# Each turn of the probabilities paired with a ternary product, and its scaling moved ahead of the sums, in an attention and ternary feed-forward kernel

## What is computed

```python
q = x + braak_embed[stage][..., None]            # one bias for each row
attn = softmax(einsum('bsd,btd->bst', q, f))     # scores against f, softmax over t
y = einsum('bst,btd->bsd', attn, f)              # the same f as values
xh = y @ H                                       # Hadamard matrix, 256 x 256
scale = clip(max|xh| over the row, 1e-5) / 7
xq = clip(round(xh / scale), -8, 7) * scale      # 4-bit codes
wq = ternary(weight) * mean|weight| of its row   # -1, 0, 1
out = x + einsum('bsi,oi->bso', xq, wq)
```

## Time and profile before

| | |
|---|---|
| median of three runs | 104.96 us |
| span of the profiled execution, first to last instruction | 102.9 us |
| rest of the time, before and after the span | 2.1 us |
| PE busy (matmul) | 96.4 us, 94% |
| PE's weight loads | 91.0 us, 88% |
| DVE busy | 87.0 us, 85% |
| ACT busy | 76.2 us, 74% |
| POOL busy | 48.5 us, 47% |
| DMA transposes of the codes | 13, 2.4 to 3.8 us from issue to landing |

### The profile page before, as it was taken

How to read it: one execution, slowest core, us unless ns; L and a number is a source line. 1 busy time by engine, 2 the same in 40 slices (tenths; PEclk the granted TensorE clock), 3 DMA queues, 4 the chain that set the end, 5 groups by cost and what they waited for, 6 DMA issues and landing times.

```text
span 102.9 us, 2603 instructions
## 1 busy us (share of the span) xinstructions
PE 96.4 (94%) x801; PEld 91.0 (88%) x801; DVE 87.0 (85%) x221; ACT 76.2 (74%) x196; POOL 48.5 (47%) x72
## 2 busy tenths in 40 slices
PE   5999999999999999999999999999999999999640
PEld 2579899999999999999999999999999999899420
DVE  1067898899989898999989998989899998988881
ACT  3354878878796978787878889697978784786820
POOL 5144499804443435354545454343435454505880
PEclk9999999999999999999999999999999999999995
DMA  2896721326269464838282735546472121221126
GB/s 68 294 275 162 274 83 68 135 51 204 51 210 157 171 188 113 244 31 289 52 300 51 273 84 204 153 155 202 114 242 79 44 63 71 51 102 48 54 102 204
DMA packets 14718, 14.70 MB, mean 143 GB/s; under 512 B 7922, under 2 KB 8824, under 8 KB 14712
## 3 DMA queue, kind: packets, MB, share of 16 engines
q1 hardware_dynamic: 14400, 14.36, 46.8%
q10 hardware_dynamic: 312, 0.27, 0.8%
HBM read 8.72 MB, written 4.19 MB: 126 GB/s over the span
## 4 chain that ended last, share of the span: by engine, by line
PE 86%; DVE 6%; ACT 3%; issue 1%; DVEq 0%
PE score_bank L477 21%; PE xh_bank L477 19%; PE fh_bank L477 14%; PE prob_bank L466 7%; PE q_bank L466 6%; PE f_bank L466 6%; PE out_bank L535 6%; PE out_bank L443 3%; ACT prob L697 2%; DVE xh_bank L1016 1%; DVE last_result L1022 1%; DVE abs_max L996 1%; PE q_bank L477 1%; PE f_bank L477 1%; DVE abs_max L984 1%
## 5 line engine op out<-in xcount | busy, mean ns | idle before, releaser
L356 POOL TENSOR_TENSOR result<-scaled,x_all 128x512 f32<-128x512 f32 x13 | 16.6, 1280 | 21.4 <-DVE scaled L854 20.8
L348 POOL TENSOR_TENSOR code<-code,magic 128x512 bf16<-128x512 f32 x13 | 13.6, 1043 | 12.1 <-ACT code L675 12.1
L691 ACT CAST fh_hi<-fh_bank 128x512 fp32r<-128x512 f32 x16 | 9.4, 589 | 8.6 <-PE fh_bank L477 8.6
L697 ACT ACTIVATE prob<-score_bank,neg_max 128x256 f32<-128x256 f32 x30 | 14.0, 478 | 1.1 <-DVE neg_max L897 1.1
L477 PE MATMUL fh_bank<-had,f_hi 128*128 128x256 f32 x64 | 14.0, 300 | 0.0
L868 DVE TENSOR_TENSOR prob_lo<-prob_bank,prob_hi 128x512 fp32r<-128x512 f32 x16 | 11.0, 690 | 3.3 <-ACT prob_hi L687 3.3
L477 PE MATMUL score_bank<-f_hi,q_hi 128*128 128x256 f32 x60 | 13.2, 302 | 0.0
L675 ACT ACTIVATE code<-xh_bank,inv_scale 128x256 f32<-128x256 f32 x30 | 12.7, 481 | 0.3 <-DVE inv_scale L851 0.2
L477 PE MATMUL fh_bank<-had,f_lo 128*128 128x256 f32 x64 | 12.8, 282 | 0.0
L666 ACT CAST f_hi<-f_bank 128x512 fp32r<-128x512 f32 x15 | 8.8, 588 | 4.5 <-PE f_bank L466 4.4
L477 PE MATMUL xh_bank<-fh_hi,prob_hi 128*128 128x256 f32 x60 | 12.1, 283 | 0.0
(11 more groups left out here) (148 smaller groups left out, 236.0 us busy)
## 6 DMA issues: line engine op xcount, KB each, us to landing
f_nat<-f_dram SPq DMA_DIRECT2D x16, 256.0 KB, 2.8
x_all<-x_dram SPq DMA_DIRECT2D x16, 256.0 KB, 3.0
out_dram<-result SPq DMA_DIRECT2D x14, 256.0 KB, 2.0
w_raw<-weight_dram SPq DMA_DIRECT2D x1, 256.0 KB, 5.0
out_dram<-result SPq DMA_DIRECT2D x2, 128.0 KB, 1.8
out_dram<-last_result ACTq DMA_DIRECT2D x2, 128.0 KB, 1.8
code_t<-code SPq DMA_TRANSPOSE x13, 2.5
had_block<-hadamard_dram SPq DMA_DIRECT2D x1, 64.0 KB, 3.1
```

The costliest lines, as they stand in the source:

```text
L348: nc.gpsimd.tensor_tensor(as_rows(code16[:, b.k]), as_rows(code), magic[:, :].broadcast_to([P, W]), ALU.subtract).then_inc(code16_ready, 1)
L356: nc.gpsimd.tensor_tensor(result[:, b.k], as_rows(scaled[:, b.k]), x_all[:, b.at], ALU.add).then_inc(result_ready, 1)
L691: nc.scalar.copy(fh_hi[:, b.k], fh_bank[:, :, :]).then_inc(fh_hi_ready, 1)
L697: a = nc.scalar.activation(prob[:, t], score_bank[:, t], ACT.Exp, bias=neg_max[:, b.k, t:t + 1], accum_out=row_sum[:, b.k, t:t + 1])
```

## The change

PE: `turn_prob` of batch i-2 and `times_ternary` of batch i-4 become one stage, `turn_prob_beside_ternary`. It turns one 128x128 block, issues one 128x256 ternary product, and so four times. The wait for the turned codes and for the free `out_bank` stands behind the first turn. The ternary product thereby moves from behind the scores to ahead of them. DVE: `scale_out` moves from behind `maximum` to ahead of `sums`. The tail is as before. Cut to its core:

```diff
+            def turn_prob_beside_ternary(b, earlier):
+                may_turn_prob(b)
+                for t in range(T):
+                    for c in range(C):
+                        turned = turn_one(prob_bank, prob, t, c)
+                        if t == c == 0:
+                            may_times_ternary(earlier)
+                        if t == T - 1 and c == C - 1:
+                            turned.then_inc(prob_in_bank, 1)
+                        mm = ternary_block(out_bank, t, c, earlier)
+                mm.then_inc(out_in_bank, 1)
+
+            def step(batch, before_mix=lambda: None):
+                if b := batch(LAG_LOAD_TURN):
+                    turn_f(b)
+                    turn_q(b)
+                b, earlier = batch(LAG_MIX), batch(LAG_OUT)
+                if b and earlier:
+                    turn_prob_beside_ternary(b, earlier)
+                elif b:
+                    turn_prob(b)
+                if b := batch(LAG_SCORE):
+                    score(b)
+                    times_hadamard(b)
+                before_mix()
+                if b := batch(LAG_MIX):
+                    mix(b)
...
             STAGES_IN_ORDER = (
                 (scales, LAG_QUANT), (split_f, LAG_LOAD_TURN), (split_q, LAG_LOAD_TURN),
-                (split_prob, LAG_MIX), (sums, LAG_MIX), (maximum, LAG_SCORE),
-                (scale_out, LAG_OUT), (split_fh, LAG_SCORE))
+                (split_prob, LAG_MIX), (scale_out, LAG_OUT), (sums, LAG_MIX),
+                (maximum, LAG_SCORE), (split_fh, LAG_SCORE))
```

More of the change, by code:

```diff
@@ L489, in turn_q, with turn_one, may_turn_prob, turn_prob @@
                 turn(q_bank, q_nat[:, b.k], ident[:, :]).then_inc(q_in_bank, 1)
-            def turn_prob(b):
+            def turn_one(to, of, t, c):
+                return pe.transpose(to[:, c, t * P:(t + 1) * P], of[:, t, c * P:(c + 1) * P],
+                                    ident[:, :])
+            def may_turn_prob(b):
                 wait(pe, prob_ready, b.at + 1)
                 wait(pe, prob_lo_ready, b.at)
+            def turn_prob(b):
+                may_turn_prob(b)
                 turn(prob_bank, prob, ident[:, :]).then_inc(prob_in_bank, 1)
@@ L531, in mix, with ternary_block, may_times_ternary, times_ternary @@
                 product(xh_bank, mixed(b)).then_inc(xh_in_bank, 1)
+            def ternary_block(to, t, c, b):
+                return pe.matmul(to[:, t], code_t[:, b.k, t, c], tern_t[:, c],
+                                 start=c == 0, stop=c == C - 1)
             def ternary_tile(to, t, b):
                 for c in range(C):
-                    mm = pe.matmul(to[:, t], code_t[:, b.k, t, c], tern_t[:, c],
-                                   start=c == 0, stop=c == C - 1)
-                return mm
[L539 to L543, removed]
+                    mm = ternary_block(to, t, c, b)
+                return mm
+            def may_times_ternary(b):
+                wait(pe, code_turned[b.k], 16 * b.half + 16)
                 wait(pe, scaled_ready, b.at)
+            def times_ternary(b):
+                may_times_ternary(b)
                 for t in range(T):
@@ L598, in _ @@
             mix(b0)
[L599 to L603, removed]
+            step(peeled(3), before_mix=weights)
             pe.wait_ge(tern_t_ready, 1)
```

## The result

The changed kernel takes 106.41 us (median of five runs, 105.83 to 108.2) against 104.96: slower, ratio 1.0121 with a 95% interval of 1.0089 to 1.0153, that is +1.27 us (+0.9 to +1.6) where I had forecast +2.9. The sign and the range held, the size did not. Some executions of either kernel take some 2 us longer than the rest; the ratios compare the others alone.

A forecast was written before the change was run, and what follows sets the result against it. PE was taken as the bound, busy 96.4 of 102.9 us. Terms of 0.54 + 1.93 + 0.43 = 2.90, added to the median 104.96, gave 107.9 us, with a range of 105.4 to 108.6.

The forecast's parts named there:

- term 1: PE, steps 4 to 15: alternating turns and ternary products adds three change-overs of 0.015 us per step, +0.54.
- term 2: PE, steps 4, 6 and 8: the ternary product needs its codes 1.8 us sooner and waits for late transposes, +1.93.
- the bounds: PE change-overs from turn to ternary product: from costing nothing (-0.18) to as much as after scores (+0.54, taken).
- The lower bound of -0.18: PE, twelve steps: bf16 weights cost nothing after a turn, so one change-over of 0.015 per step is saved.
- What the pairs do not do: PE pairs: alternating hides no weight loads, since turns are set by their moving side; 0.109 + 0.109 either way.
- don't speed it: SP's queue: result stored some 0.8 us earlier and loads go earlier, without making the codes' DMA transpose faster.
- the tie to PE's loop: Steps 6 and 8: instruction fetches delaying transposes come where PE enters its loop and first jumps back, so they return.
- Term 3: DVE scaling ahead of the maximum: exponentials end 0.43 us later, free in the loop, +0.43 at the turn after step 15.
- rival 3: Exponentials become the bound in each step: a later DVE maximum brings waits in 12 steps, +0.6, 108.5 us; 12%.

The follow-up runs named there:

- e5: Kernel before, with the four ternary products each set behind one of the last four score products instead of one block behind them; ratio 1.0068 to the kernel before.
- e3: Changed kernel with four turns in one block, then four ternary products in one block, still ahead of the scores; 106.0 us, ratio 1.0107.
- e4: Changed kernel with the pairs' ternary products reading constant zeros, so not waiting for the DMA transpose, which still runs; ratio 1.0025.
- e9: Changed kernel traced again without an edit; 106.13 us, ratio 1.0147.
- e1: Changed kernel with the scaling put back behind the maximum on DVE, PE's pairs kept; ratio 1.0098 to the kernel before.
- e6: Changed kernel with steps 6 and 7 written out, so every engine's loop begins at step 8; ratio 1.0103.
- e2: Kernel before with only the scaling moved ahead of the sums, PE's order unchanged; 105.19 us, ratio 1.0050.
- e8: Changed kernel with constant codes (no wait for the transpose) and the scaling back behind the maximum; ratio 0.9984.
- e11: Changed kernel with the scaling put back, steps 4 to 9 written out in the old order and pairs only in steps 10 to 15; 105.31 us, ratio 1.0056.
- e10: e1 run again beside e9 on the same chip; median 106.58 us, ratio 1.0118.

## Why the prediction was right and wrong

Of the 1.63 us between +2.90 and +1.27, term 1 makes 0.70 and term 2 0.93. Two steps failed: a price carried over to a place where it does not hold, and the length of two landings taken as fixed.

**Term 1 failed: +0.54 said, -0.16 measured.** The step of it that failed is the choice between the bounds. I took the row of bf16 weights behind an fp32r product for a turn, because it was the nearest row. It was near in type only. Of the turn itself I had read from the rows that its product starts 0.05 behind its load, where fp32r products come 0.12 apart, which should have made me doubt that a bf16 load is held behind it as well. e5 shows the hold-back to be there behind fp32r products (0.018 each), the changed kernel's 0.11 shows it absent behind turns. The lower bound of -0.18 was nearly right: 12 x -0.013 is -0.16.

**What the pairs do not do** was right: the load at 92.17 against the product at 92.22 said that turns are not bound by their weights, and e3 gives the same step with blocks. One of the rows beside it I misread: at 4.94 the weights are 6 x 128 and not 128 x 128, so whether loads set the 0.12 of the fp32r products stays argued. The Trainium skill ("TensorE: Matmul & The Clock Gate", LDWEIGHTS) gives one figure for a load of 128 columns, an estimate of 107 ns. The turns' own 0.109 would fit it, but by it the ternary product beside a turn would have hidden about half of the load; the pairs at 0.11 and 0.11 show that nothing was hidden, and the measurement decides.

**Term 2 was the right mechanism at the wrong size: +1.93 said, 1.0 (e4) to 1.19 (e9) measured.** Steps 4, 6 and 8 are the ones that wait, as said. Step 4 cost 0.20 in e9 (0.18 said). Steps 6 and 8 cost 0.36 and 0.63 (0.81 and 0.94 said, after the 0.045 is taken off). The step that failed: I took the transposes' 3.7 and 3.8 us as fixed. In the changed kernel they took 3.1 and 3.4 (e9), 0.6 and 0.4 less, where the losses came out 0.45 and 0.31 smaller:

```profile
30.90 1.97 SPq L285 DMA_TRANSPOSE code_t<-code  x1
code_t<-code SPq DMA_TRANSPOSE x1, 3.1
...
42.39 1.68 SPq L285 DMA_TRANSPOSE code_t<-code  x1
code_t<-code SPq DMA_TRANSPOSE x1, 3.4
```

I also said that the earlier stores and loads "don't speed it". Over all traces it looks otherwise: with the scaling early the two disturbed transposes took 3.26 in the mean (12 of them, in six traces), with the scaling late 3.6 (14 in seven). In the traces the 16 KB fetch begins 0.2 to 1.0 after the transpose's issue in the first group and 0.6 to 1.3 after it in the second. It is no rule for a single one: the longest, 4.0 in e1, has its fetch 0.6 behind the issue. That is an association in one trace of each variant; no run took the fetch away or moved it alone, so why the landings became shorter, which engine fetches, and why the fetch comes sooner stay open. And the tie to PE's loop, by which I expected the fetches to come back, was wrong in its reason (e6) though they did come back.

**Term 3 was right: +0.43 said, 0.44 in the rows, +0.3 to +0.8 in e2.** The exponentials in the loop had just the slack that the shift takes: rival 3 did not come about, though nothing is left over: in e9 they end at 62.27 and the turn's weights load at 62.32, the 0.05 of a signal later.

**The sum:** -0.16 + 1.0 + 0.43 = 1.27 against 2.90. It closes by construction, since the 1.0 is itself a difference of two measured times. What tests it is that e4 without landings measured 0.26 for -0.16 + 0.43, that e8 without either measured -0.17 for -0.16, and that the rows of e9 give 1.43 for a span longer by 1.42. The times of e4 and e8 are uncertain by 0.3 to 0.4 us each; the rows are sharper, but they are those of one execution.

## What to carry to other kernels

Moving a consumer ahead on a full engine spends the slack of everything that it waits for, and the median of a DMA's time doesn't tell whether it is enough: compare the new need with each single landing, and with the latest. Before alternating two kinds of products to hide weight loads, look for a product whose load starts just ahead of it: if it isn't delayed, there is nothing to hide. A price measured at one change-over belongs to the pair of instructions at which it was measured.

## What the runs showed of the hardware that I had not expected

- A bf16 weight load does not run ahead under an fp32r product (load and product both start at 57.85 in e5; 0.018 us lost at each change-over and return), but does under an fp32 turn (load at 62.42, product at 62.53 in e9; 0.11 from turn to product).
- A DMA transpose beside which a single 16 KB instruction fetch runs lands 0.3 to 1.5 us later than the others: all 26 such transposes of the thirteen traces took 2.8 to 4.0, while the rest took 2.4 to 2.6, but for one of 2.9 (e11). By how much differs from trace to trace, though the fetch itself is of the same size. That the fetch is the cause is argued from this, no run took it away. The two variants with more steps written out show new fetches (e6, e11).
- With PE exposed to such a landing, executions of one kernel spread further: e10 from 105.2 to 106.8, where those of the kernel before, measured beside it, lie from 104.4 to 105.0.
